# Expert tiles of 128 rows in pairs, and three blocks of batches instead of two

## What is computed

```python
def _L1_ffn_ref(x, gate_w, gate_b, w1, b1, w2, b2):
    TOP_K = 2
    xf = x.reshape(b * t, d)
    scores = xf @ gate_w + gate_b
    topk_s, topk_i = jax.lax.top_k(scores, TOP_K)
    comb = jnp.zeros_like(scores).at[jnp.arange(n)[:, None], topk_i].add(topk_s)
    h = jnp.maximum(jnp.einsum('nd,edh->neh', xf, w1) + b1, 0.0)
    eo = jnp.einsum('neh,ehd->ned', h, w2) + b2
    out = jnp.einsum('ne,ned->nd', comb, eo)
x = x + _L1_ffn_ref(_layernorm(x, axis=-1), ...)
```

## Time and profile before

| | us |
|---|---|
| Three executions | 2931.30, 2927.97, 2929.44 |
| Median | 2929.44 |
| The profiled execution, its own time | 2933.47 |
| Its span, first to last instruction | 2931.6 |

### The profile page before, as it was taken

How to read it: one execution, slowest core, us unless ns; L and a number is a source line. 1 busy time by engine, 2 the same in 40 slices (tenths; PEclk the granted TensorE clock), 3 DMA queues, 4 the chain that set the end, 5 groups by cost and what they waited for, 6 DMA issues and landing times. The chain is left out here.

```text
span 2931.6 us, 49210 instructions
## 1 busy us (share of the span) xinstructions
PE 2398.4 (82%) x16164; PEld 1880.4 (64%) x16164; DVE 1984.3 (68%) x4760; ACT 1442.5 (49%) x2778; POOL 1361.2 (46%) x1281
## 2 busy tenths in 40 slices
PE   5888888399999479999999999868888775399880
PEld 3666666389999346566556566547777664399870
DVE  4888888466555268888878888726777665377783
ACT  3666666255555257777777777633333231222220
POOL 5777777454342354444444444114555555000475
PEclk9999999699999789999999999779999897699995
DMA  2222221332220001001001010022222222544795
GB/s 67 62 69 72 59 73 48 75 127 92 61 86 26 29 19 34 26 30 33 26 30 34 26 30 26 19 97 76 90 91 90 91 86 71 164 140 138 222 299 159
DMA packets 205352, 226.68 MB, mean 77 GB/s; under 512 B 32511, under 2 KB 190209, under 8 KB 204849
## 3 DMA queue, kind: packets, MB, share of 16 engines
q1 hardware_dynamic: 181712, 170.85, 18.8%
q0 software_dynamic: 22016, 50.58, 5.5%
q10 hardware_dynamic: 1376, 2.10, 0.2%
HBM read 131.99 MB, written 95.49 MB: 78 GB/s over the span
## 5 line engine op out<-in xcount | busy, mean ns | idle before, releaser
L1320 POOL TENSOR_TENSOR f_hm<-f_hm,f_mhalf 128x64 f32<-128x64 f32 x32 | 347.4, 10855 | 2.7
L1488 DVE TENSOR_REDUCE f_nm<-f_raw 128x4 f32<-128x1024 f32 x256 | 311.9, 1218 | 33.6 <-PE f_raw L1588 33.5
L1381 ACT ACTIVATE f_PT<-f_sco 128x1024 f32<-128x1024 f32 x256 | 262.6, 1026 | 84.6 <-PE f_sco L1606 81.4
L2325 POOL DMA_INDIRECT d_pick<-expert_out,e_out_slots x128 | 131.4, 1027 | 286.2 <-DMA expert_out<-d_eo 233.0
L1588 PE MATMUL f_raw<-f_k4T,f_q4T 64*128 64x256 f32 x1024 | 142.1, 359 | 37.7 <-DVE f_nm L1488 36.9
L895 ACT ACTIVATE b_hT<-b_H,b_b1r 128x512 f32<-128x512 f32 x128 | 88.4, 690 | 163.0 <-PE b_H L1024 147.8
L2344 ACT ACTIVATE d_hh<-d_H 128x512 fp32r<-128x512 f32 x78 | 46.6, 598 | 244.8 <-PE d_H L2438 244.8
L1588 PEld LDWEIGHTS f_raw<-f_k4T,f_q4T 64*128 64x128 f32 x1024 | 85.9, 207 | 106.0 <-DVE f_nm L1488 54.2
L1818 POOL DMA_INDIRECT expert_in<-g_xm,e_slots x128 | 128.6, 1005 | 39.6 <-issue 36.9
L1039 PE MATMUL b_O<-b_w2l,b_hTh 128*128 128x256 f32 x512 | 144.9, 283 | 0.0
L1039 PE MATMUL b_O<-b_w2h,b_hTl 128*128 128x256 f32 x512 | 144.7, 283 | 0.0
(11 more groups left out here) (364 smaller groups left out, 7868.2 us busy)
## 6 DMA issues: line engine op xcount, KB each, us to landing
d_xs<-expert_in SPq DMA_DIRECT2D x78, 256.0 KB, 3.1
expert_out<-d_eo SPq DMA_DIRECT2D x78, 256.0 KB, 2.2
x_scratch<-a_x SPq DMA_DIRECT2D x64, 256.0 KB, 2.7
b_w<-in_L_ffn_W_dram SPq DMA_DIRECT2D x16, 1024.0 KB, 5.7
a_x<-in_x_dram SPq DMA_DIRECT2D x32, 256.0 KB, 3.7
a_cx<-in_ctx_dram SPq DMA_DIRECT2D x32, 256.0 KB, 3.1
f_x<-x_scratch SPq DMA_DIRECT2D x32, 256.0 KB, 2.7
f_xr<-x_scratch SPq DMA_DIRECT2D x32, 256.0 KB, 2.7
```

Of the source, the lines that this page charges most:

```text
L1320: g.tensor_tensor(hm[b % 2][:, :], hm[b % 2][:, :], mhalf[:, :], ALU.pow).then_inc(hroot, 1)
L1381: s.activation(PT[n % 3][:, t, :, :], heads(SCO), ACT.Exp, scale=float(DH) ** -0.5).then_inc(probs_ready, 1)
L1488: v.tensor_reduce(nm[:, t, g * HG:(g + 1) * HG], heads(RAW), AX.X, ALU.max, negate=True)\
L2325: g.indirect_dma_start(pick[b % GR][:, t, c, :], None, ex.eo_d[k], bass.IndirectOffsetOnAxis(ap=ex.out_slots[:, b, t, c:c + 1], axis=0), b ...
```

## The change

A tile has 128 rows. Tiles are taken in pairs, and each half of a pair has its own expert and row number; the work of a pair in the loop has the size of one tile before. The blocks are 16, 10 and 6 batches, with 72, 48 and 32 tiles, so 36, 24 and 16 pairs, 76 in all. SyncE loads a pair with two DMAs. The merges of a block start three pairs into the next and come every 1.5 pairs; the last block's 6 batches (and one of the middle block) are merged after the last pair.

```diff
-        self.BLOCKS = (B - B // 3, B // 3)
-        self.NE, self.TILE = NE, 2 * P
+        self.BLOCKS = (B // 2, B // 2 - B // 5, B // 5)
+        self.NE, self.TILE, self.PAD = NE, P, 2 * P
         most = max(self.BLOCKS) * S
-        self.region = most + self.TILE
-        self.stride = NE * self.region + (NE - 1) * self.TILE
-        self.tiles = [2 * n * S // self.TILE + NE - 1 for n in self.BLOCKS]
+        self.region = most + self.PAD
+        self.stride = NE * self.region + NE * self.TILE
+        self.tiles = [2 * ((2 * n * S // self.TILE + NE) // 2) for n in self.BLOCKS]
...
-    TILES = [(k, j) for k, n in enumerate(ex.tiles) for j in range(n)]
-    N = len(TILES)
+    PAIRS = [(k, j) for k, n in enumerate(ex.tiles) for j in range(0, n, T)]
+    N = len(PAIRS)
...
-                if k + 1 < len(ex.BLOCKS):
-                    ready_after.append(first[k + 1] + 2 + b * (ex.tiles[k + 1] - 3) // n)
-                else:
-                    ready_after.append(N)
+                after = ready_after[-1] + 1.5 if ready_after else 0
+                ready_after.append(min(N, max(after, sum(pairs[:k + 1]) + 3)))
...
-                row = sync.value_load(ex.row[k][0:1, j:j + 1], min_val=0, max_val=ROWS - ex.TILE)
                 if m >= XR:
                     sync.wait_ge(xT_psum, m - XR + 1)
-                sync.dma_start(xs[m % XR][:, :, :], ex.xs_d[bass.ds(row, ex.TILE), :]
-                               .rearrange("(t p) d -> p t d", p=P)).then_inc(xs_loaded[m % XR], 16)
+                for t in range(T):
+                    row = sync.value_load(ex.row[k][0:1, j + t:j + t + 1], min_val=0, max_val=ROWS - ex.TILE)
+                    sync.dma_start(xs[m % XR][:, t, :], ex.xs_d[bass.ds(row, ex.TILE), :]).then_inc(xs_loaded[m % XR], 16)
...
-                v.tensor_tensor(up_sb[m % 2][:, :, :], halves(UB[m % 2]),
-                                b1[:, bass.ds(e, 1), :].broadcast_to([P, T, D]), ALU.add).then_inc(up_ready, 1)
+                for t, e in enumerate(es):
+                    last = v.tensor_tensor(up_sb[m % 2][:, t, :], halves(UB[m % 2])[:, t, :],
+                                           b1[:, bass.ds(e, 1), :].rearrange("p o d -> p (o d)"), ALU.add)
+                last.then_inc(up_ready, 1)
...
-            def product(bank, high, low, n, e):
-                for t in range(T):
+            def product(bank, high, low, n, es):
+                for t, e in enumerate(es):
...
-            def expert_of(m):
-                k, j = TILES[m]
-                return pe.value_load(ex.expert[k][0:1, j:j + 1], min_val=0, max_val=NE - 1)
+            def experts_of(m):
+                k, j = PAIRS[m]
+                return [pe.value_load(ex.expert[k][0:1, j + t:j + t + 1], min_val=0, max_val=NE - 1) for t in range(T)]
```

More of the change, by code:

```diff
@@ L1756, in _ @@
             for k in range(NB_):
-                at, spare = ex.base[k] + NE * ex.region, (NE - 1) * ex.TILE
+                at, spare = ex.base[k] + NE * ex.region, NE * ex.TILE
                 sync.dma_start(ex.xs_d[at:at + spare, :].rearrange("(n p) d -> p n d", p=P),
@@ L2249, in experts_phase @@
         x5_rows, out_rows = rows(ex.x5_d), rows(out.rearrange("b s d -> (b s) d"))
-        first = [sum(ex.tiles[:k]) for k in range(len(ex.tiles))]
+        pairs = [n // T for n in ex.tiles]
         ready_after = []
@@ L2254, in experts_phase @@
             for b in range(n):
-                if k + 1 < len(ex.BLOCKS):
-                    ready_after.append(first[k + 1] + 2 + b * (ex.tiles[k + 1] - 3) // n)
-                else:
-                    ready_after.append(N)
+                after = ready_after[-1] + 1.5 if ready_after else 0
+                ready_after.append(min(N, max(after, sum(pairs[:k + 1]) + 3)))
+        ready_after = [int(m) for m in ready_after]
         merged_after = lambda m: [b for b in range(B) if ready_after[b] == m]
@@ L2315, in _ @@
             for k, n in enumerate(ex.BLOCKS):
-                done = first[k] + ex.tiles[k]
+                done = sum(pairs[:k + 1])
                 for r in range(ER):
@@ L2369, in x_low @@
                     .then_inc(xT_ready, 1)
+            def experts_of(m):
+                k, j = PAIRS[m]
+                return [dve.value_load(ex.expert[k][0:1, j + t:j + t + 1], min_val=0, max_val=NE - 1) for t in range(T)]
             def add_b1(m):
-                k, j = TILES[m]
-                e = dve.value_load(ex.expert[k][0:1, j:j + 1], min_val=0, max_val=NE - 1)
+                es = experts_of(m)
                 dve.wait_ge(up_psum, m + 1)
@@ L2390, in add_b2 @@
                     dve.wait_ge(eo_stored[m % ER], 16 * (m // ER))
-                v.tensor_tensor(eo[m % ER][:, :, :], halves(OB[m % 2]),
-                                b2[:, bass.ds(e, 1), :].broadcast_to([P, T, D]), ALU.add).then_inc(eo_ready, 1)
+                for t, e in enumerate(es):
+                    last = v.tensor_tensor(eo[m % ER][:, t, :], halves(OB[m % 2])[:, t, :],
+                                           b2[:, bass.ds(e, 1), :].rearrange("p o d -> p (o d)"), ALU.add)
+                last.then_inc(eo_ready, 1)
             def merge(b):
@@ L2442, in xT @@
             def xT(m):
-                pe.wait_ge(xs_loaded[m % XR], 16 * (m // XR + 1))
+                pe.wait_ge(xs_loaded[m % XR], 16 * T * (m // XR + 1))
                 if m >= 2:
@@ L2461, in product, with experts_of @@
                 return last
-            def expert_of(m):
-                k, j = TILES[m]
-                return pe.value_load(ex.expert[k][0:1, j:j + 1], min_val=0, max_val=NE - 1)
+            def experts_of(m):
+                k, j = PAIRS[m]
+                return [pe.value_load(ex.expert[k][0:1, j + t:j + t + 1], min_val=0, max_val=NE - 1) for t in range(T)]
             def up(m):
-                e = expert_of(m)
+                es = experts_of(m)
                 pe.wait_ge(xT_ready, m + 1)
@@ L2471, in up @@
                     pe.wait_ge(up_ready, m - 1)
-                product(UB[m % 2], xh[m % 2], xl[m % 2], 0, e).then_inc(up_psum, 1)
+                product(UB[m % 2], xh[m % 2], xl[m % 2], 0, es).then_inc(up_psum, 1)
             def down(m):
-                e = expert_of(m)
+                es = experts_of(m)
                 pe.wait_ge(hT_ready, m + 1)
@@ L2478, in down @@
                     pe.wait_ge(eo_ready, m - 1)
-                product(OB[m % 2], hh[m % 2], hl[m % 2], 1, e).then_inc(out_psum, 1)
+                product(OB[m % 2], hh[m % 2], hl[m % 2], 1, es).then_inc(out_psum, 1)
             pe.wait_ge(consts, 2)
```

6 lines of the change are left out of this document (3 added, 3 removed).

## The result

| | before, us | after, us |
|---|---|---|
| Median | 2928.70 (2925.18 to 2931.30, 4 runs) | 3019.85 (3018.47 to 3022.87, 4 runs) |
| Ratio | | 1.0313, 95% interval 1.0297 to 1.0329 |
| Profiled span | 2931.6 | 3018.0 |

The change makes the kernel 91 us slower, 3.1%. The forecast was 2992, +63, with a range of 2945 to 3040. All times in this document are of fast executions; one slow one, 3686.7 us of the second kernel with three blocks alone, is left out.

A forecast was written before the change was run, and what follows sets the result against it. The prediction took TensorE's array as the expert stage's bound, with PE's sequencer becoming it after the change. Terms +25.6 + 2.4 + 56.3 - 21.2 = +63.1 us on a 2929.44 median gave 2992 us, range 2945 to 3040.

The forecast's parts named there:

- Third term: Expert loop: added reads and address steps make PE's sequencer the bound, 4.95 us a pair, 0.3 a merge; +56.3 us.
- The bounds on record for a read: PE's number reads in the loop: 0.47 to 0.95 us each around the 0.65 taken; -27 and +46 us.
- rival of hidden register work: Expert loop: PE's register work stays hidden, 3.79 us a pair and 1.07 a merge; 2923 us, faster; chance 0.06.
- First term: Third block's added seam in the cross-attention pass: tables and 16 pads hold up the next batch; +25.6 us.
- The rival in which the seam is free: Cross-attention pass: pads fall where GpSimd is not waited for; 2967 us; chance 0.04.
- Second term: Expert stage's start: SyncE issues four row loads instead of two ahead of the weights; +2.4 us.
- Tail: After the last matmul: six batches left instead of ten, 16 gathers fewer at 1.33 us; -21.2 us.
- A second read half hidden: PE's reads in the loop: a second adds 0.3 us, 4.25 a pair, VectorE's loop next at 4.4; 2958 us; chance 0.20.
- The clock: Expert loop: TensorE's clock falls for a quarter of the time, 5.42 us a pair; about 3027 us; chance 0.12.

The follow-up runs named there:

- second kernel with three blocks alone: Second run of the kernel before, 256-row tiles with one expert, only its blocks changed to 16, 10 and 6 batches: 3046.78 us, ratio 1.0216.
- runs with 8 pads: The change with numbers read once per pair per engine, no bounds steps, and 8 pad DMAs at a block's end instead of 16: 3000.69 and 2997.45 us.
- pe_one: The change, but TensorE reads only the first half's expert number and uses it for both halves in both products: 2965.05 us, ratio 1.0129.
- shared: The change, same result, but TensorE reads a pair's two expert numbers once and keeps them for the second product: 2966.27 us, ratio 1.0124.
- second lean run: The change with each number read once per pair on TensorE and VectorE, without bounds steps, 16 pads, second run: 3034.12 us, ratio 1.0171.

## Why the prediction was right, and where it was off

**Right in sign and place.** PE's sequencer is the new bound. Three pieces of evidence settle it: with its register work alone the kernel before has pairs of 5.42 us as the change has 5.38, without VectorE's part the change keeps them (5.39), and with two reads less on PE they fall to 4.47.

**Third term, +56.3 forecast, +84.4 measured.** The term is half as large again as forecast, and the step that was mis-sized is the price of a read. The prediction took every read at 0.65; the four of a pair take 2.93 us together and not 2.60. Of that, 0.28 is the first of the two ahead of d_O, whose load takes double in every pair: 76 x 0.28 = 21 us. The sixteen address steps take 2.00 instead of 1.92 (+6). With all of it a pair is 5.38 in the median, 0.43 over the 4.95, or 33 us for 76. The bounds on record for a read, 0.47 and 0.95, hold the mean of the two added ones, about 0.79. The merges gave 3 us back: from d_hl to d_hl, 51 pairs without a merge at a mean of 5.11 and 24 with one at 6.13 are 408 us, 4 more than 75 at 5.38. That is 0.17 a merge, against 0.3 forecast, so a merge is covered as said.

The 1.07 of the earlier trace rows was one tile. Over the loop of the kernel before, 327.1 - 78 x 3.79 = 31.5 us for 22 merges is 1.43 each. The forecast does not use it, but the rival of hidden register work does: at 1.43 it would have stood near 2932 us, no change, and not at 2923.

**First term, +25.6 forecast, +23.1 measured.** The seam is as in the earlier trace rows. Its two steps are 27.5 us over two normal ones of 14.15 in the first and 24.2 in the second; before's are 26.5 over (the 14.64 of the prediction is the mean of three steps, one of them 15.6). The cross pass came out only 20.1 longer because steps of 15.6 us, which before has six times, stand there three times, and 3.0 came at its end. So the term's size is in part luck. The rival in which the seam is free is refuted. The runs with 8 pads show that nearly all of the pads' time is on the path.

**Second term, +2.4 forecast, -0.4 measured.** The weights are issued 2.5 us later after the first row load, as said, but the first d_H does not come later. From the weights' issue to the first d_H it was 31.6 us and is 28.7; what gave the 2.9 us back was not looked into.

**Tail, -21.2 forecast, -21.7 measured.** It is as said.

**The rivals.** *Register work hidden* is refuted by the kernel before with this work: +91 us. The page "Advanced Engine Details and Errata" of the Trainium skill, section Sequencer and Instruction Queues, says that instructions queue while a control instruction executes. The trace agrees in part: of the reads ahead of d_U only 0.15 us a pair reach TensorE. But the sequencer's sum of 5.4 us stays, and the rest of it shows ahead of d_O. *A second read half hidden* would have given 4.25 to 4.4 a pair. A load behind another costs its full 0.3 plus the steps, and one of the four costs double. The pace named there for VectorE's loop, 4.4, is what pe_one and shared show (4.35 and 4.47), so the next bound was rightly placed. *The clock* is refuted: 1.00 at 79% busy in the loop. The page "DMA: Bandwidth & Descriptors" of the Trainium skill, section Latency and other measured facts, gives a floor of about 600 ns for a tensor load. The traces do not bear it out as a floor, since three of four loads take 300 ns; the fourth takes 574 to 612. By its price the forecast was 3038, by the trace's 2992, and 3020 came.

## What to carry to other kernels

Add up an engine's sequencer time per iteration, with every read of a number, address step and semaphore, and compare the sum with the array's time per iteration: as soon as it is larger, "issue" shows up ahead of matmuls, and each further read costs its full time. (The other way round, taking reads out helps only down to the next bound: 1.6 us less on PE gave 0.9 here.) When work gets finer so that parts of it have their own addresses, read each number once, keep it in a register for all uses, and drop tests that the data makes unnecessary; here that took a pair from 5.38 to 3.96 us. And where a gain comes from a shorter tail, price the seam that it needs: 16 small indirect DMAs cost 20 us, as much as the tail gave, and with both put right the kernel in two blocks is 25 us faster than in three.

## What was not expected of the hardware

- One of four loads of a number in a pair takes 574 to 612 ns, the others 295 to 308. In every kernel with four loads a pair on PE it is a quarter of them (28 of 112 in the change), and with two loads a pair in the one-number kernel none from 2580 to 2730 (69 of 69 at 301 to 310 ns). What makes it double is open: it is the one behind a product's address steps and ahead of another load.
- TensorE's clock stays at 1.00 with 0.96 us of idle time in each 5.4 us. The cross pass was granted 0.97 before and 0.94 after, busy 217.90 and 196.89 of 250, and after the change the loss stands at the seam: 0.74 from 2230 to 2280, where TensorE is busy 27.20 of 50, and 0.99 from 2050 to 2200. In the same way the held pairs of the later chips cost clock. After 6.2 us without work the four d_H transposes at 2862.17 take 1.12 us instead of 0.66. The two merge stretches, second lean run and shared kernel:

```profile
2740.00:2970.00 230.00, 148.69 (x1028) 141.66 (x1029) 121.65 (x279) 36.93 (x64) 89.08 (x88) 0.85 0.57 173
2754.00:2920.00 166.00, 138.30 (x1058) 125.90 (x1056) 122.99 (x288) 35.84 (x66) 88.45 (x88) 1.00 0.79 243
```

- Chips differ by 1.8% in the kernel before, 2930 against 2983 us. In the kernels profiled on the slower ones the extra time stands in one stretch, the pairs beside long rows of gathers, where semaphore raises are recorded up to 12.9 us late; the kernel before was not profiled there.
